# Transposes of the layer norm's tiles in step 2, softplus in eight pieces over two iterations, the end in fourteen stages

## What is computed

```python
x = x + attn(layernorm(x))      # a state-space layer (SSD)
x = x + xattn(layernorm(x))     # attention over 16-wide heads, keys and values from ctx
x = x + ffn(layernorm(x))       # low-rank experts, top 2 of 4

# attn: proj = input @ in_proj_w.T  ->  gate (8192), xBC (8192 + 1024 + 1024), dt (128)
xBC = silu(conv1d(xBC, 4 taps) + conv_b)
dt  = softplus(dt + dt_bias)
cum = cumsum(dt * -exp(A_log))               # over a sequence of 64, per head
y   = sum_j (C_i . B_j) * exp(cum_i - cum_j) * dt_j * x_j + D * x
g   = y * silu(gate);  g = g * rsqrt(mean(g*g over a group) + eps) * norm_w
out = g @ out_w.T
# ffn: logits = x @ Wr.T; gates = softmax of the top two; mid = x @ A; delta = gates * mid @ B
```

## Time and profile before

| | |
|---|---|
| median of three runs | 3079.14 us (3079.08 to 3081.07) |
| the profiled execution | 3077.76 us |
| its span, first to last instruction | 3075.9 us |
| TensorE busy | 2920.1 us, 95% |
| VectorE / ScalarE / GpSimd busy | 66% / 44% / 41% |
| mean granted TensorE clock | 0.971 of full speed |
| loop ends, waves begin | about 2948.8 us |

### The profile page before, as it was taken

The page is one execution under the profiler, slowest core; times in us unless marked ns, Lnnn a source line. Parts: engine busy times, 40 slices in busy tenths (PEclk is TensorE's granted clock), DMA queues, the critical chain, the costliest instruction groups (busy, mean ns, idle before and its releaser), DMA issues.

```text
span 3075.9 us, 56304 instructions
## 1 busy us (share of the span) xinstructions
PE 2920.1 (95%) x22224; PEld 2302.2 (75%) x22224; DVE 2041.4 (66%) x3144; ACT 1364.1 (44%) x2025; POOL 1250.0 (41%) x820
## 2 busy tenths in 40 slices
PE   3999999999999999999999999999999999999965
PEld 2777777777778777787877778787777878777744
DVE  4677777877666657866665666866566666666654
ACT  3555555555444444444344344344434434443421
POOL 2665666665333423333333333333333333333330
PEclk7999999999999999999999999999999999999975
DMA  5787777777555655565665555455566555555400
GB/s 184 244 268 263 248 260 248 239 261 264 188 184 169 187 175 167 174 184 174 200 185 178 176 184 176 156 185 182 174 199 189 168 182 186 181 177 180 152 14 14
DMA packets 179267, 578.27 MB, mean 188 GB/s; under 512 B 25216, under 2 KB 31872, under 8 KB 170816
## 3 DMA queue, kind: packets, MB, share of 16 engines
q1 hardware_dynamic: 179008, 574.66, 58.6%
HBM read 460.29 MB, written 114.29 MB: 187 GB/s over the span
## 4 chain that ended last, share of the span: by engine, by line
PE 90%; DVE 4%; ACT 3%; issue 2%; DMA 1%; POOL 0%; SPq 0%; ACTq 0%; DVEq 0%; POOLq 0%
PE p_in L431 52%; PE p_out L431 22%; PE p_y L431 10%; PE p_in L510 4%; PE p_y L601 1%; DVE cv L1121 1%; ACT L761 1%; ACT w_ring L761 0%; DVE o_ring L1063 0%; DVE xnb L1044 0%; DVE sc L1259 0%; DVE mx L1266 0%; ACT xnb L761 0%; DVE cpar L1104 0%; ACT g_sq L761 0%
## 5 line engine op out<-in xcount | busy, mean ns | idle before, releaser
L431 PE MATMUL p_in<-xnb,w_ring 128*128 128x512 f32 x6912 | 1746.1, 403 | 13.5 <-DVE cv L1121 9.3
L431 PEld LDWEIGHTS p_in<-xnb,w_ring 128*128 128x128 f32 x6912 | 1271.3, 190 | 289.1 <-issue 14.4
L1446 POOL TENSOR_TENSOR g_lo<-g_f,g_hi 128x512 fp32r<-128x512 f32 x256 | 372.4, 1455 | 1304.5 <-ACT g_hi L761 1304.5
L1121 DVE SCALAR_TENSOR_TENSOR cv<-p_in,cpar,cv 128x504 f32<-128x504 f32 (+2 forms) x960 | 702.7, 732 | 117.4 <-ACT cv L761 93.5
L431 PE MATMUL p_out<-o_ring,g_hi 128*128 128x512 f32 x2048 | 646.1, 396 | 0.0
L761 ACT ACTIVATE cv<-p_in,cpar 128x512 f32<-128x512 f32 x320 | 247.9, 777 | 759.0 <-PE p_in L431 713.8
L1156 DVE SCALAR_TENSOR_TENSOR t_y<-x_t,dpar,p_y 128x256 f32<-128x256 f32 x512 | 222.7, 476 | 406.4 <-PE p_y L431 404.3
L431 PEld LDWEIGHTS p_out<-o_ring,g_hi 128*128 128x128 f32 x2048 | 381.4, 187 | 90.9
L761 ACT ACTIVATE sg<-p_in 128x512 f32<-128x512 f32 x256 | 153.6, 600 | 658.9 <-PE p_in L431 658.9
L431 PE MATMUL p_out<-o_ring,g_lo 128*128 128x512 f32 x1024 | 404.5, 395 | 0.0
L1145 DVE TENSOR_TENSOR x_tok<-p_in,dts 128x512 f32<-128x512 f32 x256 | 176.7, 690 | 307.6 <-PE p_in L510 304.3
(11 more groups left out here) (233 smaller groups left out, 2260.5 us busy)
## 6 DMA issues: line engine op xcount, KB each, us to landing
w_ring<-ws_scr SPq DMA_DIRECT2D x432, 512.0 KB, 3.4
o_ring<-ows_scr SPq DMA_DIRECT2D x192, 512.0 KB, 3.4
ws_scr<-w_ring SPq DMA_DIRECT2D x144, 512.0 KB, 5.0
decay<-cum_scr SPq DMA_DIRECT2D x128, 512.0 KB, 6.7
raw_w<-wt SPq DMA_DIRECT2D x144, 256.0 KB, 4.2
ows_scr<-o_ring SPq DMA_DIRECT2D x64, 512.0 KB, 6.2
raw_o<-owt SPq DMA_DIRECT2D x64, 256.5 KB, 5.4
acb<-x SPq DMA_DIRECT2D x3, 1024.0 KB, 7.9
```

The lines of the kernel that those rows point to most:

```text
L431: return nc.tensor.matmul(o, lhsT=l, rhs=r, start=first, stop=last)
L1121: ins = V.scalar_tensor_tensor(acc[:, :, t:SEQ], src[:, :, 0:SEQ - t], cpar[:, 5 * m + 3 - t:5 * m + 4 - t], acc[:, :, t:SEQ], ALU.mult, A ...
L1446: T(g_lo[:, c % 2, :], g_f[:, c % 2, :], g_hi[:, c % 2, :].bitcast(F32), ALU.subtract).then_inc(glo_done, 1)
```

## The change

Nothing is computed in another way; instructions change their place.

1. The layer norm's tile: moments from early(1) to late(0), normal from step 2 to step 1, the transposes, high and low from slot 3 to slot 2; deviation moves to the front of GpSimd's list.
2. The softplus: before, part 3 in late(0), parts 4 to 7, 8 and 9, 10 and 11 in early(1) to early(3), 12 in late(4) and 13 in early(6), all in iteration 5. After: 3, 4 to 6, 7 and 8, 9 at steps 2, 3, 6, 7 of iteration 5 and 10, 11, 12, 13 at those of iteration 6. The store of cum moves from iteration 6 to 7.
3. The end: 14 stages instead of 10, and the loop tile enters at stage 9.

```diff
--- before.py
+++ after.py
@@ -221,13 +221,13 @@
             return t - 1 if t is not None and t >= 1 else None
 
         LOOP_TILES = QT * (NTB - 1)
-        STAGES = 10
+        STAGES, LATE = 14, 9
 
         def waves(stage):
 
             for w in range(STAGES + QT - 1):
-                if STAGES - 2 + w < STAGES:
-                    stage(STAGES - 2 + w, LOOP_TILES - 1, loop_tile, p_y[:, 0, :], p_y[:, 1, :])
+                if LATE + w < STAGES:
+                    stage(LATE + w, LOOP_TILES - 1, loop_tile, p_y[:, 0, :], p_y[:, 1, :])
                 for q in range(QT):
                     if 0 <= w - q < STAGES:
                         y0, y1 = ((p_in[0][:, :], p_in[1][:, :]), (p_out[0][:, :], p_out[1][:, :]),
@@ -362,7 +362,7 @@
                     sp.wait_ge(y_done, CPG * n)
                     load_decay(tb, g, 1)
                 for step in range(-1, CPG):
-                    if step == 0 and is_at(tb, g, 6):
+                    if step == 0 and is_at(tb, g, 7):
                         store_cum(tb + 1)
                     if step == 1 and first_g and tb >= 2:
                         sp.wait_ge(x2_done, QT * (tb - 1))
@@ -519,7 +519,7 @@
                     pe.wait_ge(mid_done, t)
                 if k == 2 and is_at(tb, g, 4):
                     pe.wait_ge(dtr_done, tb + 2)
-                if k == 3 and coming(tb, g) is not None:
+                if k == 2 and coming(tb, g) is not None:
                     pe.wait_ge(xl_done, coming(tb, g) + 1)
                 if k == 4 and t is not None:
                     pe.wait_ge(qtc_done, t + 1)
@@ -741,15 +741,17 @@
                     attention_in(t, S, y0, y1)
                 if k in (2, 3):
                     scores(t, S, k - 2, (y0, y1))
-                if k in (5, 6):
-                    probs(t, S, k - 5, (y0, y1))
-                if k == 7:
+                if k in (6, 7):
+                    probs(t, S, k - 6, (y0, y1))
+                if k == 8:
                     values(t, S, y0)
-                if k == 8:
+                if k == 9:
                     experts_in(t, S, y0)
+                if k == 10:
                     low_rank(t, S, y0)
-                if k == 9:
+                if k == 12:
                     gated(t, S, y0)
+                if k == 13:
                     delta(t, S, y0)
 
             waves(stage)
@@ -989,15 +991,17 @@
 
                 if k == 1:
                     attention_in(t, S, y0, y1)
-                if k == 4:
+                if k == 5:
                     soft_exp(t, S)
-                if k in (5, 6):
-                    probs(t, S, k - 5, (y0, y1))
-                if k == 8:
+                if k in (6, 7):
+                    probs(t, S, k - 6, (y0, y1))
+                if k == 9:
                     features(t, S, y0)
+                if k == 10:
                     middle(t, S, y0)
-                if k == 9:
+                if k == 11:
                     gate_exp(t, S)
+                if k == 12:
                     middle_by_rank(t, S, y0)
 
             waves(stage)
@@ -1186,15 +1190,12 @@
 
                 t, u, tile = opening(tb, g), closing(tb, g), coming(tb, g)
                 S = loop_tile
-                if k == 1 and tile is not None:
-                    dve.wait_ge(xt_in, 16 * (tile - QT + 1))
-                    moments(tile, xt[:, :])
                 if k == 2 and t is not None:
                     if t == 0:
                         dve.wait_ge(post_const, 16 * 7)
                     dve.wait_ge(acc_done, GROUPS * tb)
                     moments_of(S, acb[:, (tb - 1) % 2, t % QT, :]).then_inc(var1_done, 1)
-                if k == 2 and tile is not None:
+                if k == 1 and tile is not None:
                     normal(tile, xnt[:, :], xt[:, :], tile)
                 if k == 3 and former(t) is not None:
                     logits(t - 1, S)
@@ -1208,10 +1209,10 @@
                     softplus(tb + 1, (2,))
                 if k == 7 and t is not None:
                     maxima(t, S)
-                if is_at(tb, g, 5) and k in (1, 2, 3):
-                    softplus(tb + 1, ((4, 5, 6, 7), (8, 9), (10, 11))[k - 1])
-                if is_at(tb, g, 5) and k == 6:
-                    softplus(tb + 1, (13,))
+                if is_at(tb, g, 5) and k in (2, 3, 6, 7):
+                    softplus(tb + 1, {2: (3,), 3: (4, 5, 6), 6: (7, 8), 7: (9,)}[k])
+                if is_at(tb, g, 6) and k in (2, 3, 6, 7):
+                    softplus(tb + 1, {2: (10,), 3: (11,), 6: (12,), 7: (13,)}[k])
                 if k == 5 and u is not None:
                     sums(u, S)
                 if k == 7 and u is not None:
@@ -1224,17 +1225,16 @@
                 S = loop_tile
                 if k == 0 and former(t) is not None:
                     expert_row(t - 1, S)
-                if k == 3 and tile is not None:
+                if k == 0 and tile is not None:
+                    dve.wait_ge(xt_in, 16 * (tile - QT + 1))
+                    moments(tile, xt[:, :])
+                if k == 2 and tile is not None:
                     tok = slice((tile % QT) * P, (tile % QT + 1) * P)
                     low(tile, xnb[(tb + 1) % 2][:, 1, :, tok], xnb[(tb + 1) % 2][:, 0, :, tok], y1)
                 if k == 4 and is_at(tb, g, 4):
                     softplus(tb + 1, (0, 1))
                 if k in (5, 6) and t is not None:
                     scored(t, S, k - 5, (y0, y1))
-                if k == 0 and is_at(tb, g, 5):
-                    softplus(tb + 1, (3,))
-                if k == 4 and is_at(tb, g, 5):
-                    softplus(tb + 1, (12,))
                 if k == 2 and former(u) is not None:
                     result(u - 1, S, y0)
                 if k == 6 and u is not None:
@@ -1403,18 +1403,19 @@
                     query(t, S, x1)
                 if k in (2, 3):
                     scored(t, S, k - 2, (y0, y1))
-                if k == 3:
+                if k == 4:
                     maxima(t, S)
-                if k == 5:
+                if k == 6:
                     sums(t, S)
-                if k == 7:
+                if k == 8:
                     attended(t, S, y0)
                     residual(t, S, x1)
-                if k == 8:
+                if k == 9:
                     expert_row(t, S)
-                if k == 9:
+                if k == 11:
                     logits(t, S)
                     experts(t, S)
+                if k == 13:
                     result(t, S, y0)
 
             waves(stage)
@@ -1510,6 +1511,8 @@
                     inverse_rms(n - 1)
                 t, u = opening(tb, g), closing(tb, g)
                 S = loop_tile
+                if coming(tb, g) is not None:
+                    deviation(coming(tb, g))
                 if u is not None:
                     shifted(u, S)
                 for k in range(1, CPG):
@@ -1522,8 +1525,6 @@
                     g_low(k - 1, n)
                     if k >= 2:
                         sum_squares(k - 1, n)
-                    if k == 1 and coming(tb, g) is not None:
-                        deviation(coming(tb, g))
                     if k == 1:
                         differences(tb, g, 1, n)
                     if k == 2 and t is not None:
```

## The result

The changed kernel takes 3009.59 us (median of four runs, 3009.14 to 3010.04) against 3079.11 us for the kernel before in the same rounds: a ratio of 0.9774, 95% interval 0.9757 to 0.9791, faster by 69.5 us. The prediction was 3016 us, 2999 to 3037, from a gain of 62.4. The profiled execution took 3009.73 us, its span is 3007.9, 68.0 less than before.

A forecast was written before the change was run, and what follows sets the result against it. TensorE is busy 95% of the span, so time is won only where it waits or runs slowly: layer norm, softplus, end. Gains of 18.4 + 17 + 4 + 23 = 62.4 us gave 3016 us, range 2999 to 3037.

The forecast's parts named there:

- What bounds the kernel: TensorE is busy 95% of the span; time can be won at the layer norm's tiles, the softplus and the end.
- Part 1: Layer norm's tile one step earlier: TensorE's waits for xnb in the loop go, gaining 18.4 us.
- The sentence on GpSimd's power: Layer norm: the power now waits for moments ahead of g_low(0), which waits for ScalarE anyway; priced at nothing.
- Rival 2: Layer norm: the wait moves along with the tile because the copy is late at step 2 too; 3029 us, chance 0.08.
- Part 2: Softplus spread over iterations 5 and 6: gains 17 us in passes 2 and 3, 4 us in the first.
- Rival 3: Softplus only moves its waits: pieces behind the clamp hold x_tok in every pass; 3029 us, chance 0.11.
- Part 3: The end in more stages with the loop tile entering later: gains 23 us, between 14 and 32.
- (a): The end: tile 0's query no longer stands behind the loop tile's result on VectorE and starts 8.5 us earlier.
- (b): The end: gated, delta and result become separate stages behind expert_row, so three late waves shorten, gaining 19 us.
- (c): The end: four more waves; the last tile must let older tiles' gated and delta pass, costing 4.5 us.
- Rivals 1 and 4: End: added waves each cost what a late wave did, 3109 us, chance 0.04; or end gives half, 3028 us, 0.10.
- Rival 5: The end runs at the higher clock, about 10 us shorter still: 3006 us, chance 0.07.

The follow-up runs named there:

- the combination: The kernel after with first-pass softplus moved off steps 2 and 6, experts_in one stage later and the query one stage earlier: 2983.68 us.

## Why the prediction was right, by its steps

**What bounds the kernel: right.** The three places gave all of the gain, each by itself, as the runs with one part alone show. The mechanisms were right in all three; what was off was the size of single terms.

**Part 1, right in its mechanism, 18.4 us predicted, 23.2 measured, above its bounds of 12 to 19.4.** The waits on xnb went as said, in the first pass to 0.5 us a tile where I had 0.25, and no new wait stands before heads(2) in passes 2 and 3. Undersized was the term of the removed wait: it was priced as the wait alone, and the upper bound was the sum of the waits. The matmuls at the lower clock behind two of them gave 1.2 and 1.6 us, and the wait of 0.46 us before to_tokens(2) in each of the first pass's four went too. The sentence on GpSimd's power was right that its new place costs nothing and left out what its old place would have cost. The 1.51 us that normal took at step 2 were its 0.54 and a hold-up beside GpSimd's g_low, 1.29 us long and begun 0.07 us earlier; the prediction took them as its length, which changed no term. Rival 2 is refuted.

**Part 2, 21 us predicted, 19.5 measured.** Passes 2 and 3: 17 predicted, 17.2 measured. The first pass: 4 predicted, 2.3 measured. Its single waits were foreseen well: 3.6, 1.8 and 0.7 us, measured 3.20, 1.80 and 0.64; the pair behind the clamp took 3.48 us, as in the earlier trace rows. What was left out is again the clock, 0.98 in that iteration. Rival 3 is refuted for passes 2 and 3. (Its price was slack: new waits of 5 us in each of three passes would have left 27.8 - 15 = 12.8 us of Part 2, not 8.)

**Part 3, 23 us predicted, 25.9 measured.** (a) 8.5 predicted for query 0, 6.1 measured. The order did what was said: query 0 starts as soon as the power is done. But in this profile the last matmuls of the output projection ran slowly (0.63 us for one that took 0.39 before), and the loop tile's experts_in stands 8.6 us behind the last msv, where it stood 6.2 before; with experts_in later it stands at 6.2 again, query 0 at 7.8, and the gain is 16.3 - 7.8 = 8.5. (b) 19 predicted, 20.8 measured, with a pace of 10.25 where the lists laid side by side gave 10.3. That the split of the expert part is needed for it was shown by merging it again. The agreement of the pace is in part luck: other profiles with the same instructions there have 9.2 to 10.1. (c) 4.5 predicted, 3.65 measured. The 2.7 us between query 0 and the first experts_in were not in the sum. From the loop tile's experts_in to the last result it is 95.8 us, where I had said near 101. Rivals 1 and 4 are refuted. Rival 5 did not happen in this profile: the mean clock from the last msv to the end is 0.60 before and 0.60 after. In other executions it happened in a small part, as the wave of 7.97 us shows. That the two engines take turns in the late waves no term of the prediction looked for.

**The sum.** The errors are +4.8, -1.5, -0.6 (the last loop iteration) and +2.9: 5.6 us more than 62.4. Parts 2 and 3 are inside their ranges, Part 1 is 3.8 us above its own; the total lies within the range because the ranges of the other parts left room for it. By the means of all profiles with the old and the new end Part 3 is 28.3, 5.3 above its 23 and still inside its 14 to 32.

## What to carry to other kernels

Price a wait of TensorE with the slower matmuls that can follow it, not with its idle time alone. Where an instruction is moved, list every producer it had, and what that producer's completion sets free besides: a small power behind a gated product cost 60 us in 3010, because VectorE waited for it and because it then freed a wide GpSimd pass and a VectorE instruction that stand in each other's way. In a hand-written relay of tiles look for two engines that take turns; putting one engine's item a stage later than its producer gave here 15.4 us, more than half of what fourteen stages had given, with one line. And before a difference of a few microseconds is put down to an edit, compare stretches with the same instructions in several runs.

## What the hardware showed that was not expected

- An instruction of 0.54 us on VectorE took 3.82 us when GpSimd's 2048-column pass began 0.15 us before it, at twelve tiles of twelve.
- The clock fell after some waits and not after others of the same length: two of the eight waits of 2.09 to 2.24 us of the kernel before were followed by slow matmuls, and ten of the twelve waits of 3.14 to 3.56 us of the kernel with the power at its old place. And in some executions an iteration of the first pass takes 87.3 to 87.7 us in place of 86.2 with nothing changed in it (iteration 2 in the runs with softplus moved, with the stages merged, and with experts_in later; iteration 3 in the combination). What decides it stays open. Of any span here 1 to 1.5 us are of this kind in the loop, and up to 3.8 us behind the last msv (106.8 and 103.1 us with the same instructions).
- The late waves of the kernel after are at 0.50 of the clock in the window shown, and those of the version with a pace of 5.4 us at 1.00. But the same instructions as in the kernel after also ran at 1.00 for one wave, in the run with softplus moved. So the higher clock doesn't need the new order; whether the new order makes it more likely is open.
